# A hybrid of convolution, selective scan and attention on one core: steps ahead of VectorE's drive, expert mixing on TensorE, and bias work on ScalarE

## The reference, cut to what matters

```python
# layer 0: convolution block whose kernels are mixed from 4 experts per sample
rw = softmax(relu(pool @ r_w1.T + r_b1) @ r_w2.T + r_b2)
out = silu(bn1(einsum('oc,bchw->bohw', exp_w, x)))
kern = einsum('be,eckl->bckl', rw, dw_w)             # 576 channels, 5x5
out = silu(bn2(depthwise(out, kern)))
out = out * sc                                        # squeeze and excite
wpw = einsum('be,eoc->boc', rw, pw_w)
x = x + bn3(einsum('boc,bchw->bohw', wpw, out))
# layer 1: x + selective scan of groupnorm(x), 4 directions x 192 channels, 16 states
def step(h, inps):
    dA = exp(dt[:, :, None] * A)
    h = dA * h + (dt * u_t)[:, :, None] * B_t[:, None, :]
    y = einsum('bdn,bn->bd', h, C_t) + Dv * u_t
yh = y1 + y2 + y3 + y4
yn = (yh - mu) * rsqrt(var + 1e-05) * ln_g + ln_b
out = yn * silu(z) @ W_out
# layers 2 and 3, on tokens t = 96 channels x 784
t = t + frequency_mixer(_ln_t(t))
t = t + q_ffn(_ln_t(t))         # relu(qlinear(x, W1, b1)), then qlinear(h, W2, b2)
t = t + linear_attention(_ln_t(t))
t = t + q_ffn(_ln_t(t))
# qlinear: operands rounded to 8 bits, sums and biases to fp16
```

## Time and profile before

| | before |
|---|---|
| median of 3 runs | 26279.49 us (26266.52 to 26286.57) |
| profiled execution: its time, its span | 26389.19 us, 26387.5 us |
| mean granted TensorE clock, share of full | 0.819 |
| busy, share of the span | PE 78%, DVE 93%, ACT 44%, POOL 33% |
| DMA moved | 68 GB/s mean |
| one pass of the loop (one sample), from one start of unit 0 to the next | 405.95 us (11270.81 to 11676.76) |

### The profile page before, as it was taken

The page is one execution under the profiler, slowest core; times in us unless marked ns, Lnnn a source line. Parts: engine busy times, 40 slices in busy tenths (PEclk is TensorE's granted clock), DMA queues, the critical chain, the costliest instruction groups (busy, mean ns, idle before and its releaser), DMA issues.

```text
span 26387.5 us, 375604 instructions
## 1 busy us (share of the span) xinstructions
PE 20581.9 (78%) x125002; PEld 8812.8 (33%) x125002; DVE 24513.9 (93%) x23378; ACT 11550.1 (44%) x15421; POOL 8808.6 (33%) x4999
## 2 busy tenths in 40 slices
PE   6778778787787787877877878778778787787786
PEld 2333333333333333333333333333333333333332
DVE  5999999999999999999999999999999999999998
ACT  2444444444444444444444444444444444444443
POOL 2333333333333333333333333333333333333331
PEclk8878888888788888887888878888888788888886
DMA  2222222222222222222222222222222222222222
GB/s 74 66 71 67 68 72 62 72 69 64 71 67 68 71 62 72 69 64 71 67 67 72 62 71 70 64 71 67 67 72 62 71 69 65 71 67 67 72 62 61
DMA packets 646792, 1791.26 MB, mean 68 GB/s; under 512 B 76999, under 2 KB 87059, under 8 KB 644760
## 3 DMA queue, kind: packets, MB, share of 16 engines
q1 hardware_dynamic: 624280, 1726.94, 22.6%
q10 hardware_dynamic: 20480, 38.29, 0.5%
HBM read 1707.39 MB, written 44.96 MB: 66 GB/s over the span
## 4 chain that ended last, share of the span: by engine, by line
DVE 37%; issue 34%; PE 20%; ACT 5%; DVEq 2%; POOL 1%; DMA 0%; SPq 0%; ACTq 0%; POOLq 0%
DVE prod L1064 15%; PE bank L457 11%; DVE state L1233 9%; PE pair L457 6%; DVE drive L1064 5%; PE scan_sum L457 4%; DVE work L1064 2%; ACT work L825 1%; POOL drive L1467 1%; DVE delta L1064 1%; ACT decay L825 1%; ACT L825 1%; DVE work L1308 1%; DVE work L1332 1%; DVE pwm L1153 1%
## 5 line engine op out<-in xcount | busy, mean ns | idle before, releaser
L1467 POOL TENSOR_TENSOR drive<-du,Bb 128x784 f32<-128x784 f32 x3072 | 5964.3, 1941 | 14627.3 <-DVE drive L1064 14627.3
L457 PE MATMUL scan_sum<-prod,fold 64*64 64x392 f32 x40960 | 6452.5, 594 | 2647.4 <-DVE prod L1064 2644.8
L457 PE MATMUL bank<-pad,dg 64*64 64x392 f32 x59008 | 7515.6, 501 | 222.5 <-ACT pad L825 149.0
L825 ACT ACTIVATE decay_even<-delta,alog 128x784 f32<-128x784 f32 x3072 | 2817.9, 917 | 10807.9 <-DVE state L1233 10764.1
L1064 DVE TENSOR_TENSOR prod<-state,Cb 128x784 f32<-128x784 f32 x6144 | 6245.0, 1016 | 0.0
L1233 DVE TENSOR_TENSOR_SCAN state<-decay,drive 128x784 f32<-128x784 f32 x3072 | 5771.6, 1879 | 243.3 <-DVE pwm L1153 11.8
L1233 DVE TENSOR_TENSOR_SCAN state<-decay_even,drive 128x784 f32<-128x784 f32 x3072 | 5484.7, 1785 | 151.8 <-ACT decay_even L825 83.6
L457 PEld LDWEIGHTS bank<-pad,dg 64*64 64x64 f32 x59008 | 3410.3, 141 | 3883.7 <-issue 3103.2
L457 PEld LDWEIGHTS scan_sum<-prod,fold 64*64 64x64 f32 x40960 | 1746.3, 151 | 6143.1 <-issue 3819.4
L1064 DVE TENSOR_TENSOR drive<-du,Bb 128x784 f32<-128x784 f32 x3072 | 3006.6, 979 | 116.5 <-issue 116.5
L1410 POOL TENSOR_SCALAR_AFFINE_SELECT dg<-kern 128x640 f32<-128x640 f32 x1600 | 2542.7, 1593 | 1674.6 <-PE bank L457 1389.9
(11 more groups left out here) (176 smaller groups left out, 17363.3 us busy)
## 6 DMA issues: line engine op xcount, KB each, us to landing
Bb<-bc_rows SPq DMA_DIRECT2D x2048, 392.0 KB, 3.6
Cb<-bc_rows SPq DMA_DIRECT2D x2048, 392.0 KB, 4.2
xin<-in_x SPq DMA_DIRECT2D x64, 294.0 KB, 4.3
x_kept<-xin ACTq DMA_DIRECT2D x64, 294.0 KB, 4.6
x<-x_kept SPq DMA_DIRECT2D x64, 294.0 KB, 3.9
out_dram<-t SPq DMA_DIRECT2D x64, 294.0 KB, 2.7
crossed<-pwm ACTq DMA_DIRECT2D x128, 96.0 KB, 2.1
delta<-in_x SPq DMA_DIRECT2D x8, 1176.0 KB, 7.6
```

Of the source, the lines that this page charges most:

```text
L457: return pe.matmul(out, lhsT, rhs, start=start, stop=stop)
L825: return act.activation(out, in_, f, bias=bias, scale=scale, **more)
L1467: pool.tensor_tensor(drive[:, j % 2, :], du[:, m, :], Bb[:, q % SLOTS, :], ALU.mult).then_inc(drive_r.sem, 1)
```

## The change

Six things are done.

- `go_on` runs the steps of both generators in order of position, where before it ran all due steps of the tail and then those of `ahead`.
- On VectorE steps run at two places of a unit: those with position up to j - 0.5 behind the recurrence, the others up to j behind the product; `driving(j + 1)` comes behind both.
- The experts are mixed by TensorE: VectorE copies the shares, ScalarE makes four 128x128 matrices identity times share (`share`), TensorE multiplies them with the experts' kernels and pointwise weights (4 of 128x125 and 4 of 128x480, position 2), ScalarE copies both sums out of PSUM (position 3), and the first expansion waits for the copies.
- In `norm` TensorE multiplies with mean minus identity (`less96`), so that the product is the centred value with the sign turned; ScalarE copies it out and squares it, and VectorE has no subtraction left.
- ScalarE does the bias with ReLU of `ffn`, the down bias, and `xn1`; each waits for ScalarE's own copy before.
- The table `TAIL_AT` is another: steps up to 60 stand 2.5 to 4 units earlier, 62 half a unit earlier, 70 one and 78 0.4 later.

```diff
-TAIL_AT = ((0, 9.8), (6, 20.0), (11, 24.8), (16, 29.6), (20, 39.5), (21, 41.0), (25, 47.5), (32, 53.5),
-           (40, 61.0), (48, 71.0), (56, 80.0), (62, 83.5), (70, 89.5), (78, 95.0))
+TAIL_AT = ((0, 9.8), (6, 17.0), (11, 21.8), (16, 26.8), (20, 36.8), (21, 38.3), (25, 44.5), (32, 50.5), (40, 58.0), (42, 60.0),
+           (48, 67.5), (51, 70.5), (60, 81.0), (62, 83.0), (70, 90.6), (78, 95.4))
...
-    for s in steps:
-        while s.at <= at:
-            s.next()
+    while steps and min(s.at for s in steps) <= at:
+        min(steps, key=lambda s: s.at).next()
...
                     pe.wait_ge(x_in.sem, x_in.at(i))
-                    if later(i):
-                        pe.wait_ge(dl_a.sem, dl_a.at(i - 1))
+                    pe.wait_ge(kern_r.sem, kern_r.at(i))
                 if t == 4:
...
             def head(i):
-                yield LEAD_AT - 1
+                yield LEAD_AT - 2
+                pe.wait_ge(share_r.sem, share_r.at(i))
+                if later(i):
+                    pe.wait_ge(dl_a.sem, dl_a.at(i - 1))
+                for out, stack in ((P[0][:, 0:T0 * TAPS], dww), (P[1][:, 0:T0 * C], pww)):
+                    for e in range(E):
+                        last = mm(out, share[:, e, :], stack[:, e, :], start=e == 0, stop=e == E - 1)
+                last.then_inc(mix_mm.sem, 1)
+                yield LEAD_AT - 0.6
                 expand(i, 0)
...
                     pe.wait_ge(read.sem, read.at(i, counts[h]))
-                    mm(T[h][0:C, 0:HALF], mean96[:, :], t2[:, h * HALF:(h + 1) * HALF]).then_inc(lm.sem, 1)
+                    mm(T[h][0:C, 0:HALF], less96[:, :], t2[:, h * HALF:(h + 1) * HALF]).then_inc(lm.sem, 1)
                 yield tail_at(at + 3)
...
+            def shares(i):
+                yield 0.0
+                act.wait_ge(rwc_r.sem, rwc_r.at(i))
+                for e in range(E):
+                    ac(share[:, e, :], ident[:, :], ACT.Copy, scale=rwc[:, e:e + 1]).then_inc(share_r.sem, 1)
+
             def head(i):
+                yield LEAD_AT - 1
+                act.wait_ge(mix_mm.sem, mix_mm.at(i))
+                ac(kern[:, :], P[0][:, 0:T0 * TAPS], ACT.Copy).then_inc(kern_r.sem, 1)
+                ac(pwm[:, :], P[1][:, 0:T0 * C], ACT.Copy).then_inc(kern_r.sem, 1)
                 yield LEAD_AT
...
+                yield GATE_AT + 10.6
+                act.wait_ge(g_sh.sem, g_sh.at(i))
+                ac(xn1, xin[:, :], ACT.Identity, bias=gst[:, 7:8], scale=gst[:, 6:7]).then_inc(xn1_r.sem, 1)
                 for b in range(2):
...
             def norm(i, at, n):
-                yield tail_at(at + 2)
+                yield tail_at(at + 1.2)
                 cols = [slice(h * HALF, (h + 1) * HALF) for h in range(2)]
                 for h in range(2):
-                    act.wait_ge(lc.sem, lc.at(i, 2 * n + h + 1))
-                    ac(w[1][0:C, cols[h]], w[0][0:C, cols[h]], ACT.Square).then_inc(lq.sem, 1)
+                    act.wait_ge(lm.sem, lm.at(i, 2 * n + h + 1))
+                    ac(w[0][0:C, cols[h]], T[h][0:C, 0:HALF], ACT.Copy)
+                    ac(w[1][0:C, cols[h]], T[h][0:C, 0:HALF], ACT.Square).then_inc(lq.sem, 1)
                 yield tail_at(at + 4)
...
                         act.wait_ge(h_mm.sem, h_mm.at(i, q))
-                        ac(h16[:, m, h * HALF:(h + 1) * HALF], T[h][:, 0:HALF], ACT.Copy).then_inc(h_16.sem, 1)
+                        t = h16[:, m, h * HALF:(h + 1) * HALF]
+                        ac(t, T[h][:, 0:HALF], ACT.Copy).then_inc(h_16.sem, 1)
+                        act.wait_ge(h_16.sem, h_16.at(i, q))
+                        ac(t, t, ACT.Relu, bias=ffn_b1[f][:, m:m + 1]).then_inc(h_b.sem, 1)
                 yield tail_at(at + 14)
...
                     act.wait_ge(o_mm.sem, o_mm.at(i, 2 * f + h + 1))
-                    ac(o16[:, h * HALF:(h + 1) * HALF], T[h][0:C, 0:HALF], ACT.Copy).then_inc(o_16.sem, 1)
+                    t = o16[:, h * HALF:(h + 1) * HALF]
+                    ac(t, T[h][0:C, 0:HALF], ACT.Copy).then_inc(o_16.sem, 1)
+                    act.wait_ge(o_16.sem, o_16.at(i, 2 * f + h + 1))
+                    ac(t, t, ACT.Identity, bias=ffn_b2[f][:, :]).then_inc(o_b.sem, 1)
...
             def ahead(i):
+                yield from shares(i + 1)
                 yield from softplus(i, 4, NK, 0.4, 1.6)
...
+            go_on([Beside(shares(0))], END)
             go_on([Beside(lead(0))], END)
...
             v.wait_ge(s_par.sem, PARAMS)
+            v.tensor_scalar(less96[:, :], ident[0:C, 0:C], -1.0 / C, None, ALU.add)
             v.tensor_copy(rT2b[:, :, :], rT2[:, :].unsqueeze(2).to_broadcast([RHID, E, 128]))
...
-                link(v.tensor_copy(rwc[:, :], rw[:, i, :] if isinstance(i, int) else
-                                   rw[:, bass.ds(i, 1), :].rearrange("p b e -> p (b e)")))
-                if later(i):
-                    v.wait_ge(dw_d.sem, dw_d.at(i, 0))
-                if later(i):
-                    v.wait_ge(pw_d.sem, pw_d.at(i, 0))
-                link(v.tensor_scalar(kern[:, :], dww[:, 0, :], rwc[:, 0:1], None, ALU.mult))
-                for e in range(1, E):
-                    ins = v.scalar_tensor_tensor(kern[:, :], dww[:, e, :], rwc[:, e:e + 1], kern[:, :], ALU.mult, ALU.add)
-                    if e < E - 1:
-                        link(ins)
-                ins.then_inc(kern_r.sem, 1)
+                v.tensor_copy(rwc[:, :], rw[:, i, :] if isinstance(i, int) else
+                              rw[:, bass.ds(i, 1), :].rearrange("p b e -> p (b e)")).then_inc(rwc_r.sem, 1)
             def head(i):
-                yield LEAD_AT + 4
-                link(v.tensor_scalar(pwm[:, :], pww[:, 0, :], rwc[:, 0:1], None, ALU.mult))
-                for e in range(1, E):
-                    link(v.scalar_tensor_tensor(pwm[:, :], pww[:, e, :], rwc[:, e:e + 1], pwm[:, :], ALU.mult, ALU.add))
                 yield GATE_AT + 2.4
...
                 v.wait_ge(g_pw.sem, g_pw.at(i))
-                link(v.scalar_tensor_tensor(gst[:, 7:8], gst[:, 2:3], -1.0, gst[:, 6:7], ALU.mult, ALU.mult))
-                v.tensor_scalar(xn1, xin[:, :], gst[:, 6:7], gst[:, 7:8], ALU.mult, ALU.add).then_inc(xn1_r.sem, 1)
+                v.scalar_tensor_tensor(gst[:, 7:8], gst[:, 2:3], -1.0, gst[:, 6:7], ALU.mult, ALU.mult).then_inc(g_sh.sem, 1)
                 yield from steps(i, 0, 4, GATE_AT + 30.4, 1.0)
...
                                          ALU.mult, ALU.add).then_inc(state_r.sem, 1)
+                    go_on(between, j - 0.5)
                     if j >= 1:
                         product(j - 1)
+                    go_on(between, j)
                     if j % 2 == 1 and j + 1 < NU:
                         driving(j + 1)
-                    go_on(between, j)
                 go_on(between, END)
...
             def norm(i, at, n, out, **more):
-                yield tail_at(at + 1)
-                for h in range(2):
-                    cols = slice(h * HALF, (h + 1) * HALF)
-                    v.wait_ge(lm.sem, lm.at(i, 2 * n + h + 1))
-                    tt(w[0][0:C, cols], t2[:, cols], T[h][0:C, 0:HALF], ALU.subtract).then_inc(lc.sem, 1)
                 yield tail_at(at + 5)
                 v.wait_ge(lr.sem, lr.at(i, 2 * n + 2))
-                v.wait_ge(lc.sem, lc.at(i, 2 * n + 2))
                 alone()
...
                         t = h16[:, m, h * HALF:(h + 1) * HALF]
-                        v.wait_ge(h_16.sem, h_16.at(i, q))
-                        v.tensor_scalar(t, t, ffn_b1[f][:, m:m + 1], 0.0, ALU.add, ALU.max).then_inc(h_b.sem, 1)
                         v.wait_ge(h_b.sem, h_b.at(i, q))
...
                     cols = slice(h * HALF, (h + 1) * HALF)
-                    v.wait_ge(o_16.sem, o_16.at(i, 2 * f + h + 1))
-                    link(v.tensor_scalar(o16[:, cols], o16[:, cols], ffn_b2[f][:, :], None, ALU.add))
+                    v.wait_ge(o_b.sem, o_b.at(i, 2 * f + h + 1))
                     tt(t2[:, cols], t2[:, cols], o16[:, cols], ALU.add).then_inc(o_r.sem, 1)
...
             def ahead(i):
-                yield 0.6
+                yield -0.5
                 mix(i + 1)
...
                     if q < DRING:
-                        yield LEAD_AT - 2
+                        yield LEAD_AT
                     elif q < CONV3:
```

More of the change, by code:

```diff
@@ L40 @@
 SETUP_LINKS = 53
-LEAD_LINKS = 14
-TAIL_LINKS = 6
+LEAD_LINKS = 5
+TAIL_LINKS = 2
 DVE_LINKS = LEAD_LINKS + TAIL_LINKS
@@ L157, in build @@
         mean96 = sb("mean96", [C, C])
+        less96 = sb("less96", [C, C])
         mean192 = sb("mean192", [128, 128])
@@ L213, in build @@
         rwc = sb("rwc", [128, E])
+        share = sb("share", [128, E, 128])
         kern = sb("kern", [128, T0 * TAPS])
@@ L271, in build @@
         rw_c = sig("rw_current")
-        kern_r, pwm_r = sig("kernels_mixed"), sig("pointwise_mixed")
+        rwc_r, share_r, mix_mm, kern_r = sig("shares_read"), sig("shares_spread", E), sig("experts_mm"), sig("kernels_mixed", 2)
```

(1 more changed line is left out.)

5 lines of the change are left out of this document (2 added, 3 removed).

## The result

The changed kernel takes 26546.81 us (median of 4, 26538.56 to 26556.44) against 26276.87 us of before: ratio 1.0106, 95% interval 1.0093 to 1.0118. It is 1.1% **slower**, where 0.6% faster was forecast. Its profiled execution has a span of 26549.4 us; mean granted clock 0.833.

A forecast was written before the change was run, and what follows sets the result against it. VectorE was taken to bound the kernel. Per pass, 16.0 + 13.2 - 3.7 = 25.5 us gained, less 27.0 of new waits, plus 3.9 back, gave 2.4; times 63, 151 us, so 26130 (-0.6%), range 25450 to 26560.

The forecast's parts named there:

- VectorE's bound: VectorE sets the pass, busy 382.37 of 405.95 us, except at named waits and in a 64.50 us stretch that TensorE fills.
- the stalls behind GpSimd's drive: VectorE steps that stand still while GpSimd's drive runs; their end was to save 13.2 us per pass.
- the forecast 16.0: Work leaving VectorE, us per pass: bias with ReLU, down biases, subtractions, mixing of `pwm` and `kern`, and `xn1`.
- the 3.7: Price of steps ahead of VectorE's drive: later recurrences, 2.8 us at 23 odd units and 0.9 at five even ones.
- New waits: VectorE reaches steps sooner while ScalarE's and TensorE's chains grew: 40.6 us per pass against 13.6 before, 27.0 more.
- What comes back: Slowdown of recurrences and products while GpSimd builds diagonals, some 10.9 us per pass; a third falls into waits, 3.9 credited.
- The slower rival: Mixing and variance at 1.2 GHz throughout: wait at unit 4 13.1 instead of 8.0, time 26450 (+0.6%); chance 0.24.
- the rival's deciding 10.4: The wait at unit 4, in us, above which the prediction said the rival of 1.2 GHz throughout decides.
- the middle: Mixing time at unit 4 taken as 6.6 us, between 8.8 at 1.2 GHz and 4.4 at 2.4 GHz.
- The range's lower end: 25450 us, the forecast's case down to half of the new waits.
- the fourth rival: Gain a few times larger, with half of the new waits: 25280; it has part of the forecast case's chance of 0.54.
- The other signs: Units 0 to 5 5 us longer, units 83 to 95 some 10 shorter, 64.50 stretch unchanged, TensorE's mean clock still 0.82.

The follow-up runs named there:

- e3: The changed kernel with VectorE's steps again behind product and drive, at one place of a unit: 26954.39 us, ratio 1.0264.
- e11: The changed kernel with variance ahead of mixing and other steps repositioned, but VectorE's steps again at one place, behind product and drive: 25767.29 us, ratio 0.9805.
- e2: The kernel before with only VectorE's two places of steps and the merged order of `go_on`, no work moved: 26320.12 us, ratio 1.0024.
- e9: The changed kernel with GpSimd building only 2 of each 5 diagonal blocks, the other taps multiplied with zeros: 26174.49 us, ratio 0.996.
- e1: The changed kernel with the 192-channel LayerNorm's variance ahead of the mixing, its log and exp ahead of the delta steps': 26026.07 us, ratio 0.9916.
- e13: The e2 kernel with the mixer's first sum later and ScalarE's LayerNorm log and exp ahead of the delta steps': 26340.47 us, ratio 1.0006.

## Why the prediction was wrong

- **VectorE's bound, the stalls behind GpSimd's drive, and how they go: right.** Casts went from 598 to 357 ns, `du` from 1702 to 976, the 99x768 products from 1228 to 951; 12.8 us per pass by groups, 13.2 forecast. The groups that left were busy for 13.0, and with their own waits make some 15.3 of the forecast 16.0. VectorE's even recurrences took 1.7 more by their later start behind the drive, as part of the 3.7. VectorE's busy time is 360.8 per pass, though, where 350 to 353 was named as a sign: the forecast took idle time in the 16.0 for busy time, the 1.7 belongs to busy time, and contention rose.
- **New waits: right in sum, 27.0 forecast.** VectorE's waits of over 0.1 us are 46.0 per pass, against 22.3 and 22.1 in the two profiles of before. Of before's 22, 1.8 are the casts' waits for the bias, which the forecast had among the removed work, and 1.9 the first drive of a pass, now 0.9; without these it is 26.5 to 26.8 more. By place, forecast and measured: unit 4 8.0 and 9.4, unit 16 4.2 and 4.0, unit 26 3.0 and 4.9, units 42 and 45 5.5 and 2.4, casts at 53 to 57 3.0 and 2.1, unit 63 2.9 and 3.1, units 71 to 78 10.7 and 9.2, unit 92 2.0 and 1.9, unit 1, forecast small, 2.0.
- **"What comes back", 3.9: this step failed.** Contention was 12.6 per pass in the first profile of before and 11.9 in the second. In the changed kernel it is 14.2. The forecast took 3.9 off; it rose by 1.6 to 2.4. That is 5.5 to 6.3 us per pass, against a miss of 5.2 to 6.2 (2.4 gained was forecast, 2.8 to 3.8 lost in the traces). This one term covers the miss, while smaller misses of the others cancel. e3, e11 and e2 show where the rise comes from: from the two places. The move that ends the stalls brings the odd recurrence closer behind the drive, into GpSimd's diagonal, and the odd recurrences that a diagonal holds make 6.3 of contention per pass against 4.5 before and 4.8 in e3. Where in the pass the rise stands does not tell its cause: units 0 to 11 had 0.6 of contention before and 2.2 after, but e3 has 2.0 there too. e9 shows that the contention is real time of the pass and that waits absorb a third: the share was right, but it was taken off contention that had been in the pass before, while the change made more.
- **The slower rival: right in sign, its mechanism in part.** It wanted the mixing and the variance at 1.2 GHz throughout, a wait of 13.1 and 26450. The granted clock was 0.50 in a part of the mixing only, in every pass, and 1.00 in the variance. Mixing took 6.2 in the mean, less than the 6.6 that the forecast had taken as the middle, and the wait of 9.4 lies below the rival's deciding 10.4 in the mean, though above it in 18 of 53 passes. So the clock is not what the forecast had mis-sized. The rule of the Trainium skill ("TensorE: Matmul & The Clock Gate", What's actually happening), that the throttled 1.2 GHz is the default and activity releases it, agrees with this trace: the granted clock fell to 0.50 half a us into the mixing, behind an idle of 1.81, and was back at 1.00 while TensorE still mixed. The eight 128x480 instructions took 4.59 there, at a mean granted clock of 0.74, and 3.39 at 1.00 in e1.
- **The decision lay in one place.** e1 shows it: with the variance ahead of the mixing the change is 0.8% faster than before. The prediction priced this wait at 8.0, more than three times its net gain per pass, so that a small error anywhere else turned the sign. The range's lower end shows the same looseness: 25450 is said to stand for half of the new waits, which the fourth rival prices at 25280.
- **The other signs.** Units 0 to 5 are 8.4 longer (29.5 against 21.1), where 5 was forecast, units 83 to 95 10.8 shorter, where 10 was. The mean clock rose from 0.819 to 0.833, where no change was forecast. The full stretch, no change forecast, has 63.9 in units 67 to 83 against 63.2 and 61.8, 0.7 to 2.1 longer. What of this is the change and what the spread of before is open.
- **The median and the trace.** The medians differ by 270 us, 4.3 per pass; the traces by 2.8 and, with the second profile, 3.8. The prediction treated the first profile's 110 us as a mere offset. Most of it was a wait inside the passes: the second profile's execution is 72 us shorter, and 1.06 us per pass make 67 of them.
- **Why the places alone bring nothing** (e2, e13) is settled in part: VectorE's stalls go, and waits of the same size come at units 25 or 29 and 75 to 77, behind dependent steps and TensorE. In the changed kernel the same edit is worth 408 us. e11's casts alone name 0.68 us each, twelve times, or 8.2 per pass, more than the 6.5 that e11 lost in all, since contention gave 3.5 back.

## What to carry to other kernels

When work moves off the busiest engine, list for each of its waits what the producing engine has in front, and mend the largest in the order before judging the move: here the order of two steps was worth 520 us, and the same work is 1.1% slower in one order and 4.6% faster in another. Moving a step later pays when its operand is late by position; in the one case where it seemed late by a chain of dependent steps, the wait moved along (e13). A slowdown by contention does not come back by itself when waits grow; take credit only if the overlap itself is seen to shrink. Before steps are moved out from behind one engine's drive, look at what the other engine runs behind its own, and which instruction will now meet it: here 12.8 us of stalls went, and contention came to 1.6 to 2.4 more than before.

## What the runs showed of the hardware

VectorE's casts, products and odd recurrences that start while a GpSimd instruction runs are held until it ends, by its drive and by its diagonals alike. The cast that started in a drive took 1.76 instead of 0.36 and ended 0.22 behind it. In the 53 passes of the changed kernel 901 odd recurrences started while a diagonal was built, with 0.51 us of it left in the mean. Each ended 1.64 us behind the diagonal, all within 6 ns, so that they took 2.15 in the mean. The 106 that started first, with the diagonal beginning during them, took 1.79, like those that met none. Products ended 0.82 to 0.90 behind the GpSimd instruction that they had started in, all 2385 of them. With the shorter diagonals of e9 odd recurrences went from 1917 to 1816 ns and products from 1018 to 989.

Even recurrences, whose decays lie in PSUM, are not held: in the kernel before, 629 of them started in a drive or a diagonal of GpSimd, and took 1.77 to 1.79.

Eight 128x480 matrix instructions cost 3.39 us at a granted clock of 1.00 and 4.59 at 0.74, in two places of the order and with the same operands.
